# An attention-and-experts kernel: statistics, centring operations and TensorE's order of work rearranged inside each batch slot

## The reference

```python
# x, ctx: 16 batches of (128, 512); itok: 16 lengths
def attention(q, k, v, k_length):             # 8 heads of 16 rows, 512 queries, 512 keys
    s = SCALE * log(k_length)                 # one number per batch
    attn = softmax(s * einsum('bhdq,bhdk->bhqk', qh, kh))
    return einsum('bhqk,bhdk->bhdq', attn, vh)

def experts(x, gate_w, w1, w2, w3):           # 8 experts, 2 of them for each of 2048 rows
    probs = softmax(x @ gate_w.T); weights, index = top_k(probs, 2); weights /= sum(weights)
    h = silu(x @ w1[e].T) * (x @ w3[e].T)     # 512 -> 1024
    return sum(weights * (h @ w2[e].T))       # 1024 -> 512

x = x + attention(layernorm(x), ctx, ctx, itok)
x = x + experts(layernorm(x), ...)
```

## Time and profile before

| | |
|---|---|
| median of three runs | 1182.57 us |
| the profiled execution | 1178.09 us, its span 1176.6 us |
| TensorE's matmuls | 1033.1 us busy, 88% of the span |
| VectorE | 683.4 us, 58% |
| GpSimd | 664.4 us, 56% |
| ScalarE | 427.9 us, 36% |
| TensorE's granted clock, mean | 0.970 |

### The profile page before, as it was taken

One profiled execution on the slowest core, in us unless ns is written; L12 is line 12 of the kernel. 1 busy time (PEld: TensorE's weight loads), 2 busy tenths in 40 slices (PEclk: granted clock), 3 DMA queues, 4 the chain that ended last, 5 costly groups with the idle time before them and its releaser, 6 DMA issues.

```text
span 1176.6 us, 18912 instructions
## 1 busy us (share of the span) xinstructions
PE 1033.1 (88%) x5098; PEld 413.9 (35%) x5099; DVE 683.4 (58%) x1029; ACT 427.9 (36%) x751; POOL 664.4 (56%) x571
## 2 busy tenths in 40 slices
PE   2889999999999999851899999999999999999970
PEld 0223333333333333211344444444444444444430
DVE  5867777777777777304444545455454554544355
ACT  8267777677777777741111011011111011111110
POOL 6454777777777773232386807528383483800574
PEclk9999999999999999985999999999999999999995
DMA  6575666555556544013687656738577466733678
GB/s 198 161 224 159 185 183 181 173 178 184 177 180 180 182 146 120 31 55 90 176 227 200 189 156 168 208 79 232 156 217 170 121 191 171 206 89 89 155 207 264
DMA packets 212726, 195.84 MB, mean 166 GB/s; under 512 B 137376, under 2 KB 176288, under 8 KB 207264
## 3 DMA queue, kind: packets, MB, share of 16 engines
q1 hardware_dynamic: 197760, 122.26, 40.4%
q0 software_dynamic: 14336, 71.87, 18.5%
q10 hardware_dynamic: 576, 1.05, 0.3%
HBM read 111.48 MB, written 53.00 MB: 140 GB/s over the span
## 4 chain that ended last, share of the span: by engine, by line
PE 73%; DMA 7%; DVE 7%; issue 6%; POOL 4%; ACT 1%; POOLq 1%; SPq 0%; PEldq 0%; DVEq 0%
PE rows L1162 32%; PE heads_out L1162 15%; PE heads_out L1076 7%; PE scores L1063 7%; PE rows L1049 6%; DMA W<-parts_dram 4%; DVE nm L760 4%; POOL z L527 2%; PE misc L1126 2%; PE misc L1103 1%; PE misc L1096 1%; ACT W L642 1%; DVE st L870 1%; PE misc L1118 1%; POOL zsc L526 1%
## 5 line engine op out<-in xcount | busy, mean ns | idle before, releaser
L1162 PE MATMUL rows<-W,U 128*128 (+1 forms) x1776 | 391.0, 380 | 17.8 <-DMA U<-stage 17.1
L760 DVE TENSOR_REDUCE nm<-rows 128x2 f32<-128x1024 f32 x256 | 304.3, 1215 | 100.4 <-PE rows L1049 94.0
L642 ACT ACTIVATE W<-scores 128x512 f32<-128x512 f32 x512 | 283.4, 596 | 135.9 <-PE scores L1063 135.0
L1162 PEld LDWEIGHTS rows<-W,U 128*128 128x128 bf16 x1776 | 174.0, 98 | 228.8 <-issue 21.7
L707 ACT ACTIVATE U<-rows 128x512 f32<-128x512 f32 x78 | 46.4, 597 | 509.2 <-PE rows L1162 497.0
L1162 PE MATMUL heads_out<-W,U 128*128 x888 | 197.7, 379 | 2.2 <-DVE U L889 2.2
L1049 PE MATMUL rows<-W,U 96*128 96x512 bf16 x512 | 148.8, 400 | 49.1 <-DMA W<-parts_dram 29.1
L967 DVE TENSOR_TENSOR U<-rows,U 128x512 bf16<-128x512 f32 x78 | 53.9, 691 | 230.6 <-ACT U L707 226.3
L428 POOL TENSOR_TENSOR W<-U,W 128x2048 bf16<-128x2048 f32 x42 | 171.7, 4088 | 7.7 <-POOL W L427 7.7
L1063 PE MATMUL scores<-U,W 128*128 128x512 bf16 x512 | 168.0, 385 | 5.9 <-ACT W L642 5.2
L427 POOL TENSOR_SCALAR W<-U 128x2048 bf16<-128x2048 f32 x42 | 80.8, 1924 | 146.5 <-PE rows L1162 132.8
(11 more groups left out here) (167 smaller groups left out, 723.8 us busy)
## 6 DMA issues: line engine op xcount, KB each, us to landing
U<-wpack_dram POOLq DMA_DIRECT2D x42, 1024.0 KB, 5.9
parts_dram<-U SPq DMA_DIRECT2D x32, 384.0 KB, 4.2
U<-parts_dram SPq DMA_DIRECT2D x32, 384.0 KB, 4.1
W<-parts_dram SPq DMA_DIRECT2D x32, 384.0 KB, 5.3
stage<-slots_dram SPq DMA_DIRECT2D x39, 257.0 KB, 2.9
expert_out_dram<-U SPq DMA_DIRECT2D x39, 256.0 KB
parts_dram<-U SPq DMA_DIRECT2D x32, 256.0 KB, 4.3
stage<-wpack_dram POOLq DMA_DIRECT2D x12, 512.0 KB, 5.4
```

The source lines that it names most:

```text
L642: s.activation(probs[:, w % 2, j, kk, :], sc[u % 2][:, :], ACT.Exp) \
L760: v.tensor_reduce(nm[:, bb.parity, 2 * k:2 * k + 2], p1[k % 2][:, :].rearrange("p (c k) -> p c k", c=2), AX_X, ALU.max, negate=True).then_ ...
L1162: ins = m.matmul(bank, part_of(s_part, k), W[:, bass.ds(at_w, 512)], start=(k == 0 and n == 0), stop=(k == n_chunks - 1 and n == 2))
```

## The change

Four things are changed, all in the first part of the kernel.

1. GpSimd: z and norm are no longer made by "subtract the mean, multiply by the scale" but by "add the negated mean, multiply by the scale". The negated mean is one more 128x1 operation, issued behind the addition of epsilon without a wait between them (`two`).
2. VectorE: the input statistics stand behind reduction 4 (before: behind 5 and the reciprocals), the reciprocals behind reduction 6 (before: behind 5).
3. VectorE: the statistics of x1 stand behind reduction 14 (before: behind 13).
4. TensorE: the unit that stood at the end of steps 3 and 7 now stands in steps 2 and 6, directly behind the score; half a pass is then rows, score, score, values, score, rows, score instead of rows, score, score, values, score, score, rows. `values` is moved up in the text of the step, past small products that never stand in the same step.

```diff
-ENGINE_STEPS = {"prep": 8, "keys": 4, "z": 3, "route_a": 3, "route_b": 3}
+ENGINE_STEPS = {"prep": 9, "keys": 4, "z": 4, "route_a": 3, "route_b": 3}
...
+    def two(self, first, second):
+        first.then_inc(self.sem, 1)
+        self.done += 1
+        self.step(second)
...
-                    st.step(g.tensor_scalar(psc[:, 0:1], var, EPS, 1.0, ALU.add, ALU.mult))
+                    st.two(g.tensor_scalar(psc[:, 0:1], var, EPS, 1.0, ALU.add, ALU.mult),
+                           g.tensor_scalar(psc[:, 3:4], mean, -1.0, 0.0, ALU.mult, ALU.add))
...
-                    st.step(g.tensor_scalar(norm[:, :], xres[:, pbt.n, :], mean, psc[:, 2:3], ALU.subtract, ALU.mult))
+                    st.step(g.tensor_scalar(norm[:, :], xres[:, pbt.n, :], psc[:, 3:4], psc[:, 2:3], ALU.add, ALU.mult))
...
-                    st.step(g.tensor_scalar(zsc[:, 0:1], mv2[:, 1:2], EPS, 1.0, ALU.add, ALU.mult))
+                    st.two(g.tensor_scalar(zsc[:, 0:1], mv2[:, 1:2], EPS, 1.0, ALU.add, ALU.mult),
+                           g.tensor_scalar(zsc[:, 2:3], mv2[:, 0:1], -1.0, 0.0, ALU.mult, ALU.add))
                     st.step(g.tensor_tensor(zsc[:, 1:2], zsc[:, 0:1], mhalf[:, :], ALU.pow))
-                    st.step(g.tensor_scalar(z[:, pv.parity, 0:D], us[:, :], mv2[:, 0:1], zsc[:, 1:2], ALU.subtract, ALU.mult))
+                    st.step(g.tensor_scalar(z[:, pv.parity, 0:D], us[:, :], zsc[:, 2:3], zsc[:, 1:2], ALU.add, ALU.mult))
...
-                maxima(range(4, 6))
-                if pv.within(0, B - 1):
-                    dve.wait_ge(S["den_in"], b.n * 16)
-                    if pv.within(1, B - 1):
-                        dve.wait_ge(S["rec_out"], b.n * 16 - 16)
-                    v.reciprocal(rden[:, :], den[:, :]).then_inc(S["rec_ready"], 1)
+                maxima(range(4, 5))
...
-                maxima(range(6, 8))
+                maxima(range(5, 7))
+                if pv.within(0, B - 1):
+                    dve.wait_ge(S["den_in"], b.n * 16)
+                    if pv.within(1, B - 1):
+                        dve.wait_ge(S["rec_out"], b.n * 16 - 16)
+                    v.reciprocal(rden[:, :], den[:, :]).then_inc(S["rec_ready"], 1)
+                maxima(range(7, 8))
...
-                maxima(range(12, 13))
-                maxima(range(13, 14))
+                maxima(range(12, 15))
...
                     v.bn_aggr(mv2[:, :], st2[:, :]).then_inc(S["st2_ready"], 1)
-                maxima(range(14, 15))
...
                         if u % 4 == 0:
-                            rows_unit(4 * w + u // 2)
+                            rows_unit(4 * w + 2 * (u // 4) + 0)
                         if full:
                             score(w, u)
+                        if u in (1, 5):
+                            kk = u // 4
+                            if w == 0 and behind:
+                                values(pv, 3, kk)
+                            if w > 0 and full:
+                                values(b, w - 1, kk)
+                        if u % 4 == 2:
+                            rows_unit(4 * w + 2 * (u // 4) + 1)
...
-                        if u in (1, 5):
-                            kk = u // 4
-                            if w == 0 and behind:
-                                values(pv, 3, kk)
-                            if w > 0 and full:
-                                values(b, w - 1, kk)
...
-                        if u % 4 == 3:
-                            rows_unit(4 * w + u // 2)
```

More of the change, by code:

```diff
@@ L849, in slot @@
                     q_steps.end()
-                    v.nop().then_inc(S["prep_steps"], ENGINE_STEPS["prep"] - 3)
+                    v.nop().then_inc(S["prep_steps"], ENGINE_STEPS["prep"] - 4)
                     v.nop().then_inc(S["prep_done"], 1)
```

## The result

The changed kernel takes 1169.37 us (median of four runs, 1167.94 to 1171.74) where the kernel before takes 1181.30 beside it (median of four, 1179.75 to 1184.3): a ratio of 0.9903 [0.988, 0.9927], 11.9 us less. That lies inside the range and has the sign of the forecast. But it is close to the first rival's 11 us and not to the 17 us of the case held likeliest: the four waits go as forecast, and the reload takes part of that back.

A forecast was written before the change was run, and what follows sets the result against it. No engine is full: TensorE, in order, stops four or five times a slot for others. Per slot 0.83 + 0.68 + 0.45 + 0.2 - 0.95 = 1.2 us, 13 slots 15.7, last z 1.3: 17 us won, 1165, range 1155 to 1187.

The forecast's parts named there:

- the first rival: The mid-slot reload of the keys takes the place of the removed waits: 11 us won, 1171; chance 0.10.
- the case held likeliest: The change wins 1.2 us in each of 13 slots, the last z 1.3: 17 us, 1165; chance 0.62.
- the four waits: TensorE's waits per slot: units 7 and 8 0.83 us, maxima transpose 0.82, seam 0.68, z 0.45; together 2.8.
- The z operation: On GpSimd, z by adding a negated mean was taken at 0.61 us instead of 2.08, removing z's 0.45 us wait.
- the second rival: GpSimd's z operation stays at 2.08 us and z's wait becomes 1.48: 4 us lost, 1186; chance 0.18.
- Unit 8: TensorE's 0.83 us wait for reduction 6 goes once input statistics and reciprocals on VectorE are parted.
- the seam: Between two slots, unit 0's 0.68 us wait for reduction 14 goes with x1's statistics behind that reduction.
- the transpose of the maxima: On TensorE, its wait for reduction 11 falls from 0.82 to 0.61 us, 0.2 won.
- The waits of scores: On TensorE, scores wait 0.21 us for an exponential in five of eight half passes: 0.95 us lost a slot.
- the step that failed: Mid-slot reload of the keys on SyncE: the later reciprocals ahead of it were costed at nothing.
- signs of being wrong: z at 2 us with a long wait; reload waits in most slots; scores waiting for exponentials much longer than 0.2.
- signs of being right: z and norm about 0.6 us; units 0 and 8 unwaited; maxima transpose 0.4; scores about 0.2; period near 28.2.

The follow-up runs named there:

- The kernel that subtracts: Changed kernel with z and norm made by subtract and multiply again: 1182.16 us, ratio 1.0039 against the kernel before.
- the kernels without part 3: Changed kernel with x1's statistics back behind reduction 13, 1165.03 us, ratio 0.9888 against the kernel before; also that kernel with further edits.
- the late chunk: Changed kernel with the next weights' chunk fetched behind the reload, after the routing rows: 1166.54 us, ratio 0.9892 against the kernel before.
- the cut reload: Changed kernel with the mid-slot reload cut in two, heads 0 and 1 ahead of the reciprocals' store: 1167.15 us, ratio 0.9892 against the kernel before.
- the kernel whose only further edit is the earlier chunk: Changed kernel with x1's statistics back behind reduction 13 and the chunk fetched ahead of GpSimd's splitting: 1163.83 us, ratio 0.9874 against the kernel before.
- part 1 alone: Kernel before with only the negated mean for z and norm: 1170.32 us, ratio 0.9936.
- part 4 alone: Kernel before with only TensorE's new order: 1173.1 us, ratio 0.9955.
- parts 1 and 4: Kernel before with only the negated mean and TensorE's new order: 1163.35 us, ratio 0.9872.
- part 2 alone: Kernel before with only the input statistics ahead of reduction 5 and the reciprocals behind 6: 1192.42 us, ratio 1.0132.

## Why the prediction was right, and where its size was off

**The z operation.** Taken at 0.61 with 2.08 as the far bound, it takes 0.77, and norm the same. From scale to z it is 282.80 - 281.37 = 1.43 us, where 1.16 + 0.13 was said: the extra 128x1 operation costs 0.27 from start to start. z is done at 283.57, and the transposes, which could start at 283.11 + 0.44 = 283.55, start at 283.75: 0.2 us of z's 0.45 remain. The kernel that subtracts bears out the other end of the range: with the long operation the change loses. (By the Trainium skill, "GPSIMD Engine Reference", section "Performance pitfalls for Q7 kernels", the estimate was 1.7 us for either form. The trace has 0.77 for add-multiply and 2.08 for subtract-multiply, so the rule does not hold for this operation. With 1.7 us the prediction's own sum would have come to some 2 us won, by its 1.4 us for each 0.1, and not to the sum of the second rival, 4 us lost, as the prediction has it.)

**Unit 8, the seam, the transpose of the maxima.** Right in the slot as a whole: units 8 and 0 wait no more, the transpose's wait is hidden behind the reload's, and x1's scale starts 281.37 - 279.92 = 1.45 us behind its statistics, as said.

**The waits of scores.** Right in place, number and size: 0.21 us, five times in a slot.

**The reload: the step that failed.** Of the prediction's own signs of being wrong one came, waits for the reload in most slots, and of its signs of being right two did not: the slot is 28.89 us and not near 28.2, and the maxima's transpose shows no wait of 0.4. The time is nearer to the first rival's 1171 than to 1165; it is inside the likeliest case's own range only because that range reaches to 1171. The sum costed the move of the reciprocals and the shorter pass 2 at nothing. SyncE is in fact through in time: the reciprocals' store is issued at 266.55, ahead of the last score of pass 1. But the window shrinks to 5.5 us, as the first rival said, and transfers that take 6.3 to 7.2 us don't fit it. That rival had counted them late in some slots; they are late in eleven of thirteen. Each wait is 11.1/11 = 1.0 shown and 0.16 more for the modelled end; 0.6 of it is free, since the maxima's transpose would have waited. So 0.56 us in 11 of 13 slots, 0.47 on average; with the 0.2 left of z, 0.67. That is nearly the whole distance from 28.18 us, the slot of the kernels without part 3 where nothing waits for the reload, to 28.89. The changed kernel shows the same in itself: its last chunk is fetched at 382.1 us, and the two slots behind that (between the transposes of z at 399.40, 427.74 and 456.08) take 28.34 us each, where the ten with a chunk take 28.52 to 29.44. The kernels with the late chunk and with the cut reload, which keep part 3, have 28.34 and 28.35 in their regular slots too; the 0.16 to 28.18 fits z's remaining 0.2.

That the chunk beside the keys makes their transfer late is shown by these slots, by the kernel whose only further edit is the earlier chunk (4.9 us of waits to 1.7), and by the one with the later chunk (11.1 to 0.4). Against the transfer the prediction set that the chunk's fetch would lead by more: it does, by 1.3 to 1.6 us, as worked out, but whether a lead of so little helps the runs leave open. With part 1 alone it is some 2.1 us in most slots, and none waits for the reload, in the old order's longer window. In the new order, at a lead of mostly 0.3 to 0.6 us the kernel with part 4 alone waits 8.5 us in ten slots, and the change without part 1 waits 7.4 us in ten, less than the changed kernel's 11.1 at 1.6; at 2.6 us the wait is 4.9 in one kernel and 7.5 in another. Only the chunk at 6.9 us ahead, or behind the reload, takes the wait away.

**Which parts carry it.** Part 1 alone wins 0.64%, part 4 alone 0.45%, the two together 1.28% [1.06, 1.51]; the whole change wins 0.97% [0.73, 1.2]. The prediction gave unit 8's 0.83 us to part 2 and the seam's 0.68 to part 3. The runs show that neither is needed: in TensorE's new order alone unit 8 does not wait, and with parts 1 and 4 the seam costs 0.31 us, of which the pair behind it gives back 0.21. So TensorE's new order, with the shorter operation, wins nearly all of what the moves on VectorE were priced at, and it is also the new order that shortens the reload's window, since with it alone the reload is late in ten slots. In TensorE's old order part 2 costs 1.3%, since the reciprocals then hold up the reload. Part 3 starts z, the rest of GpSimd's work and the chunk's fetch later; by the slots that costs 0.5 us in each (28.89 against 28.41, one profiled execution of each), while in the total the intervals (0.9903 and 0.9888) don't separate the two.

Still open: whether part 2 adds anything to parts 1 and 4, and whether parts 2 and 3 together lose. The kernel with 1 and 4 and the one with 1, 2, 4 and the early chunk are level (0.9872 and 0.9874), and the intervals of parts 1 and 4 and of the whole change overlap.

## What to carry to other kernels

A wait that is removed ahead of a transfer is taken from that transfer's window: work out the window anew and hold it against the slowest transfers of the trace, not against the slots in which it happened to fit. Two moves can remove the same wait (unit 8's and the seam's here), or one be harmless only beside the other (the reciprocals in TensorE's new order), so time parts singly and in pairs before keeping all. An engine that is never waited for still issues transfers: when its work moves, its loads can move into another's way.

## What was not expected of the hardware

On GpSimd, 128x512 f32 with two operands taken per row costs 2.08 us as subtract-multiply and 0.77 as add-multiply; with constants, and a bf16 output, multiply-add costs 0.61. The pair of operations makes 1.31 us, the kind of operand and the output's type together 0.16.

The keys' transfer, the same 384 KB each time, takes between 4.65 us (at 18.28 in the kernel with part 1 alone) and 9.02 us (at 75.57 in the change without part 1) on the chains of these runs.

Behind a late reload TensorE can run at the lower level of its clock. In the profiled execution of the changed kernel a unit waits for a reload of 8.64 us, and the values behind it take 1.94 us; in the kernel before, behind a reload of 7.73, they take 1.06:

```profile
85.13 0.60 PE L1055 MATMUL rows<-W,U 96*128 96x512 bf16 x2 [2.53 <-DMA W<-parts_dram]
...
86.10 1.94 PE L1082 MATMUL heads_out<-W,U 128*32 128x512 f32 x8
```

```profile
83.06 0.60 PE L1049 MATMUL rows<-W,U 96*128 96x512 bf16 x2 [1.51 <-DMA W<-parts_dram]
...
84.03 1.06 PE L1076 MATMUL heads_out<-W,U 128*32 128x512 f32 x8
```

The granted clock from 85 to 90 us is 0.66 after the change (the column behind the five engines' busy times and counts), a mean of the two levels, 0.50 and 1.00, or 1.2 and 2.4 GHz:

```profile
85.00:90.00 5.00, 4.87 (x17) 1.65 (x18) 2.54 (x4) 1.68 (x3) 3.02 (x4) 0.66 0.47 162
```

Of the 3.0 us by which the first of z's transposes comes later, 1.0 is there ahead of this reload (the values ahead of it start at 79.08 before and 80.12 after), 1.0 is the longer wait, and the rest comes behind it.

In the first 50 us the lower level is not new with the change, though the granted clock shown from 40 to 55 us is 0.50 after the change and 1.00 before it. By the pace of their units both kernels begin at the lower level:

```profile
36.13 1.04 PE L1049 MATMUL rows<-W,U 96*128 96x512 bf16 x2 [0.18 <-DVE nm L760]
```

```profile
37.46 0.60 PE L1055 MATMUL rows<-W,U 96*128 96x512 bf16 x2 [1.44 <-DVE nm L767]
38.59 2.17 PE L1055 MATMUL rows<-W,U 96*128 96x512 bf16 x4 [0.53 <-DVE nm L767]
```

The first line is the kernel before, the others are after the change. Two products take 1.04 us at the lower level and 0.60 at the higher. The kernel before stays at the lower until about 52 us; the changed one is at the higher for a moment, from about 35 to 38 us, and then again at the lower until about 55.

In the kernel with parts 1 and 4 the lower level follows an idle 2.06 us at 241.97, and that slot takes 31.36 us. So a late reload can cost about a microsecond more than its wait. It need not, and the length of the idle time alone does not tell which: with part 2 alone an idle 2.58 us at 281.66 is followed by values at full speed (1.06 us), with part 4 alone an idle 1.78 us at 83.29 by values that take 1.51. What made the first reductions and loads fall differently in the early part was not tried, nor why single transfers are slow.
